# A radial coupling's last geometry operation moved from GpSimd to VectorE, and two vector products of two tiles made one

## The reference

```
R   = relu(edge_weight @ w1 + b1) @ w2 + b2              # 384 numbers per edge
Y   = spherical_harmonics(edge_attr_3)                   # 1, 3 and 5 of them
Fj  = x[src]                                             # 8 scalars, 8 vectors of 3
acc = acc + norm * einsum('euv,ef,evi,ofi->euo', R.., Y.., F.., C)   # for each pair of orders
out = zeros.at[dst].add(concat(msg_blocks))
x   = layernorm(x + out)
```

## Time and profile before

| | us |
|---|---|
| median of 3 timed runs | 20091.51 |
| lowest and highest | 20090.82, 20093.43 |
| span of the profiled execution | 25995.0 |
| radial stage in that span | 13880 to 21703 |

### The profile page before, as it was taken

One profiled execution on the slowest core, in us unless ns is written; L12 is line 12 of the kernel. 1 busy time (PEld: TensorE's weight loads), 2 busy tenths in 40 slices (PEclk: granted clock), 3 DMA queues, 4 the chain that ended last, 5 costly groups with the idle time before them and its releaser, 6 DMA issues.

```text
span 25995.0 us, 290953 instructions
## 1 busy us (share of the span) xinstructions
PE 9853.2 (38%) x63545; PEld 7350.7 (28%) x63546; DVE 16714.1 (64%) x23622; ACT 6288.5 (24%) x13799; POOL 13429.9 (52%) x14067
## 2 busy tenths in 40 slices
PE   0131000000000006765225666666666666324422
PEld 0131000000000006664223444444444444313421
DVE  9898574547344438888555666666666677555555
ACT  0002121112111105543002333333333345201400
POOL 0187676667777760000664555555555552363165
PEclk6555555555555559985556777777777776555555
DMA  1133434441000001116222000000000006424623
GB/s 14 25 33 27 29 31 29 29 29 13 6 6 6 6 15 48 41 52 227 69 69 18 9 10 9 9 9 9 9 9 9 9 10 144 137 64 87 205 65 61
DMA packets 1751558, 1095.98 MB, mean 42 GB/s; under 512 B 1217323, under 2 KB 1658124, under 8 KB 1750028
## 3 DMA queue, kind: packets, MB, share of 16 engines
q0 software_dynamic: 454272, 412.11, 13.3%
q1 hardware_dynamic: 1089532, 417.46, 6.8%
q10 hardware_dynamic: 207632, 265.14, 3.3%
HBM read 700.94 MB, written 391.12 MB: 42 GB/s over the span
## 4 chain that ended last, share of the span: by engine, by line
DVE 31%; another core or an unknown queue 21%; issue 17%; DVEq 12%; PE 11%; ACT 4%; DMA 2%; ACTq 1%; POOL 0%; SPq 0%; POOLq 0%
PE banks L1423 5%; DVE arena L1768 5%; DVE arena L1767 4%; DVE red L2523 4%; DVEq L2201 3%; DVE hot L2196 2%; DVE arena L1740 2%; DVE arena L2207 2%; DVE srcs L2516 2%; PE banks L1365 2%; PE banks L1410 2%; DVEq L498 1%; DVE arena L1585 1%; DVEq L2261 1%
## 5 line engine op out<-in xcount | busy, mean ns | idle before, releaser
L804 POOL DMA_INDIRECT srcs<-spread,nbx x2808 | 2653.2, 945 | 5691.9 <-issue 3372.8
L782 POOL DMA_INDIRECT gat<-tab,nbr x3328 | 3455.0, 1038 | 2537.8 <-issue 1271.9
L1423 PE MATMUL banks<-w2rows,dsts 128*128 128x384 f32 x6656 | 3443.8, 660 | 1030.2 <-DVE srcs L2516 699.0
L782 POOL DMA_INDIRECT gat<-tab,pay x3328 | 3161.6, 950 | 1077.4 <-issue 892.0
L748 POOL DMA_INDIRECT pay<-records,nbr x2560 | 2746.2, 1073 | 843.1 <-issue 827.1
L1208 PE MATMUL banks<-ident,arena 128*128 128x128 f32 x2240 | 436.2, 379 | 7154.4 <-DVE arena L1768 2837.8
L909 ACT COPY banks<-arena 128x1024 f32<-128x1024 f32 (+1 forms) x1508 | 1318.6, 875 | 6430.8 <-issue 2701.9
L2511 DVE TENSOR_TENSOR srcs<-banks,g_s 128x512 f32<-128x512 f32 x1664 | 1146.1, 689 | 2252.6 <-remote 1505.1
L1208 PEld LDWEIGHTS banks<-ident,arena 128*128 128x128 f32 x2240 | 400.7, 204 | 7190.5 <-DVE arena L1768 2844.2
L2523 DVE TENSOR_REDUCE red<-srcs 128x160 f32<-128x2560 f32 x832 | 2346.2, 2820 | 75.6
L1279 PE MATMUL banks<-srcs,hot 128*128 128x96 bf16 (+1 forms) x11232 | 1169.8, 281 | 3175.7 <-DVE hot L2196 2136.8
(11 more groups left out here) (392 smaller groups left out, 22029.8 us busy)
## 6 DMA issues: line engine op xcount, KB each, us to landing
spread<-srcs SPq DMA_DIRECT2D x936, 192.0 KB, 2.9
dsts<-key_rows SPq DMA_DIRECT2D x234, 512.0 KB, 4.1
spread<-srcs ACTq DMA_DIRECT2D x468, 204.0 KB, 2.4
staged<-gat SPq DMA_DIRECT2D x416, 148.0 KB
gat<-staged ACTq DMA_DIRECT2D x416, 148.0 KB, 2.1
dsts<-key_rows ACTq DMA_DIRECT2D x117, 512.0 KB, 4.3
gat<-tab,nbr POOLq DMA_INDIRECT x3328
gat<-tab,pay POOLq DMA_INDIRECT x3328
```

Source lines behind the costliest of these rows:

```text
L782: pool.indirect_dma_start(out=gatv(s, GC[pas])[:, t, :], out_offset=None, in_=TAB[pas], in_offset=bass.IndirectOffsetOnAxis(ap=row, axis=0 ...
L804: pool.indirect_dma_start(out=chunk_rows(s, c)[:, q, :], out_offset=None, in_=rows, in_offset=bass.IndirectOffsetOnAxis(ap=nbx[:, r, s * X ...
L1423: last = t_.matmul(bank[1 + 2 * (p % 2) + h][:, 0:384], hid_rows[:, s % 2, 2 * p + h, :], w2rows[:, :], start=True, stop=True)
```

## The change

GpSimd's geometry keeps tmpA and tmpB; the subtraction goes to VectorE, after tmpC's product and before g_s's reduction. GEO_OPS is 2, VectorE waits for `geo_ops` there, and no longer between the reduction and the first pair. A new semaphore `geo_used` tells GpSimd that VectorE has read tmpA and tmpB; GpSimd waits for it before it overwrites them. The two products of lines 2516 become one of 768 elements over both tiles, with R repeated over three components and g_v over eight channels. The vector part of a message has the component first (o, then u), also in the last product and in the sums; the two additions to x read it with a stride.

```diff
-        GEO_OPS = 3
+        GEO_OPS = 2
...
-                if stage == 0:
-                    if not first:
-                        pool.wait_ge(geo_ops, n * GEO_OPS)
-                    pool.wait_ge(geo_ready, 2 * n + 1)
-                    pool.nop(nofuse=True)
-                    g.tensor_tensor(tA, fT[:, b, :, 2:5, :], r_(b, 1), ALU.mult).then_inc(geo_ops, 1)
-                    g.tensor_tensor(tB, fT[:, b, :, 1:4, :], r_(b, 2), ALU.mult).then_inc(geo_ops, 1)
-                else:
-                    pool.wait_ge(geo_ops, n * GEO_OPS + 2)
-                    pool.nop(nofuse=True)
-                    g.tensor_tensor(g_v[:, b, :, :, 8:16], tA, tB, ALU.subtract).then_inc(geo_ops, 1)
+                if not first:
+                    pool.wait_ge(geo_used, n)
+                pool.wait_ge(geo_ready, 2 * n + 1)
+                pool.nop(nofuse=True)
+                g.tensor_tensor(tA, fT[:, b, :, 2:5, :], r_(b, 1), ALU.mult).then_inc(geo_ops, 1)
+                g.tensor_tensor(tB, fT[:, b, :, 1:4, :], r_(b, 2), ALU.mult).then_inc(geo_ops, 1)
...
+                dve.wait_ge(geo_ops, (n + 1) * GEO_OPS)
+                v.tensor_tensor(g_v[:, b, :, :, 8:16], tA, tB, ALU.subtract).then_inc(geo_used, 1)
                 dve.drain()
                 v.tensor_reduce(g_s[:, b, :, 8:16], tmpC[:, :, :].rearrange("p t (v o) -> p t v o", o=3), AX.X, ALU.add)
                 dve.drain()
-                dve.wait_ge(geo_ops, (n + 1) * GEO_OPS)
...
-                    for h in range(2):
-                        last = v.tensor_tensor(
-                            prod[:, f0 + h, 16:40, :].rearrange("p (u o) k -> p u o k", o=3),
-                            bank[lo + h][:, 256:384].rearrange("p (u a k) -> p u a k", a=1, k=16).to_broadcast([P, 8, 3, 16]),
-                            g_v[:, b, t0 + h:t0 + h + 1, :, :].to_broadcast([P, 8, 3, 16]), ALU.mult)
-                    last.then_inc(r_used, 1)
+                    v.tensor_tensor(
+                        prod[:, f0:f0 + 2, 16:40, :].rearrange("p t (o u) k -> p t o u k", o=3),
+                        banks[:, lo:lo + 2, 256:384].rearrange("p t (a u k) -> p t a u k", a=1, k=16).to_broadcast([P, 2, 3, 8, 16]),
+                        g_v[:, b, t0:t0 + 2, :, :].rearrange("p t o (a k) -> p t o a k", a=1).to_broadcast([P, 2, 3, 8, 16]),
+                        ALU.mult).then_inc(r_used, 1)
...
-            v.tensor_tensor(x[:, :, 8:F], x[:, :, 8:F], a2[:, :, 8:F], ALU.add)
+            xv = x[:, :, 8:F].rearrange("p w (u o) -> p w u o", o=3)
+            v.tensor_tensor(xv, xv, a2[:, :, 8:F].rearrange("p w (o u) -> p w u o", o=3), ALU.add)
```

More of the change, by code:

```diff
@@ L445, in resnorm_gnn_kernel @@
         geo_ops = sem("geo_ops")
+        geo_used = sem("geo_used")
         r_ready = sem("r_ready")
@@ L512, in sort_held @@
             return flat[:, lo:lo + (1 << (log - 2))].rearrange("p (x m l) -> p x m l", x=x, m=m)
-        GEO_OPS = 3
+        GEO_OPS = 2
+        tA, tB = [t[:, :, :].rearrange("p t (o v) -> p t o v", o=3) for t in (tmpA, tmpB)]
         @block.sync
@@ L810, in r_, with geometry @@
                 return rx[:, b, :, lo:lo + 3].rearrange("p t (o a) -> p t o a", a=1).to_broadcast([P, TPS, 3, 8])
-            tA, tB = [t[:, :, :].rearrange("p t (o v) -> p t o v", o=3) for t in (tmpA, tmpB)]
-            def geometry(n, s, stage, first=False):
+            def geometry(n, s, first=False):
                 b = s % 2
-                if stage == 0:
-                    if not first:
-                        pool.wait_ge(geo_ops, n * GEO_OPS)
-                    pool.wait_ge(geo_ready, 2 * n + 1)
-                    pool.nop(nofuse=True)
-                    g.tensor_tensor(tA, fT[:, b, :, 2:5, :], r_(b, 1), ALU.mult).then_inc(geo_ops, 1)
-                    g.tensor_tensor(tB, fT[:, b, :, 1:4, :], r_(b, 2), ALU.mult).then_inc(geo_ops, 1)
-                else:
-                    pool.wait_ge(geo_ops, n * GEO_OPS + 2)
-                    pool.nop(nofuse=True)
-                    g.tensor_tensor(g_v[:, b, :, :, 8:16], tA, tB, ALU.subtract).then_inc(geo_ops, 1)
+                if not first:
[4 more added lines that the diff above has]
+                g.tensor_tensor(tB, fT[:, b, :, 1:4, :], r_(b, 2), ALU.mult).then_inc(geo_ops, 1)
             def radial_gather():
@@ L836, in step @@
                     if geo:
-                        for stage in range(2):
-                            geometry(n + 1, s1, stage)
+                        geometry(n + 1, s1)
                     if gathers:
@@ L845, in radial_gather @@
                     gather_step(PASS_L2, 0, s, True)
-                for stage in range(2):
-                    geometry(0, 0, stage, first=True)
+                geometry(0, 0, first=True)
                 for s in range(SLOTS):
@@ L2524, in radial_step @@
                         dve.drain()
-                v.tensor_tensor(red[:, b, :, 41:CR].rearrange("p t (u o) -> p t u o", o=3),
-                                rx[:, b, :, 0:3].rearrange("p t (a o) -> p t a o", a=1).to_broadcast([P, TPS, 8, 3]),
-                                red[:, b, :, 0:8].rearrange("p t (u a) -> p t u a", a=1).to_broadcast([P, TPS, 8, 3]),
+                v.tensor_tensor(red[:, b, :, 41:CR].rearrange("p t (o u) -> p t o u", o=3),
+                                rx[:, b, :, 0:3].rearrange("p t (o a) -> p t o a", a=1).to_broadcast([P, TPS, 3, 8]),
+                                red[:, b, :, 0:8].rearrange("p t (a u) -> p t a u", a=1).to_broadcast([P, TPS, 3, 8]),
                                 ALU.mult).then_inc(msg_ready, 1)
@@ L2543, in _ @@
             v.tensor_tensor(x[:, :, 0:8], x[:, :, 0:8], a2[:, :, 0:8], ALU.add)
-            v.tensor_tensor(x[:, :, 8:F], x[:, :, 8:F], a2[:, :, 8:F], ALU.add)
+            xv = x[:, :, 8:F].rearrange("p w (u o) -> p w u o", o=3)
+            v.tensor_tensor(xv, xv, a2[:, :, 8:F].rearrange("p w (o u) -> p w u o", o=3), ALU.add)
             v.tensor_copy(dinv[:, :], a2[:, :, F])
             dve.drain()
-            v.tensor_tensor(x[:, :, 8:F], x[:, :, 8:F], a2[:, :, F + 1:C2], ALU.add)
+            v.tensor_tensor(xv, xv, a2[:, :, F + 1:C2].rearrange("p w (o u) -> p w u o", o=3), ALU.add)
             dve.wait_ge(tab_sent, 32)
```

## The result

The changed kernel takes 19,876.95 us (19,871.05 to 19,880.46 in four runs), the kernel before 20,091.58 us: a ratio of 0.9892, 95% interval 0.988 to 0.9904. That is 214.6 us less. The forecast was 20,062 us and its range ended at 19,905 us, so it was wrong by 185 us, and the range missed the time by 28 us.

The account below looks back on a forecast made before the run. VectorE with TensorE's waits (14.8 us a step) was taken as the pace, GpSimd (14.15 us) close behind. VectorE's terms, 0.27 - 0.09 - 0.25 = -0.07 us over 416 steps, gave 20091.5 - 29 = 20,062 us; range 19,905 to 20,145 us.

Parts of the forecast that it names:

- The recording's stalls: Profiled span: 25995.0 us against 20091.5 timed; some 5,460 us of unnamed waits taken as added by recording, not the kernel's.
- The last steps: End of the radial stage, without late gathers: 15.67 us a step less 0.9 unnamed, said to confirm 14.8 us.
- VectorE with TensorE's waits is the pace, GpSimd close behind: Radial step: VectorE 13.66 us plus 1.2 of TensorE's waits, 14.8 us; GpSimd 14.15, some 0.65 to spare.
- Rival (a): Radial step: GpSimd paces the timed runs; 0.56 us less over 384 steps, 19,877 us; chance 21%.
- a fall by over 100 us: Whole time: such a fall would make the prediction wrong and mean that GpSimd was the pace.
- I leave the sum as it is: TensorE's matmuls: bank release 0.12 us later; late third pairs lose about 0.05 instead of winning 0.07, kept for the range.
- Rival (b): TensorE falls to its low clock more often; at one step in twenty 95 us, 20,157 us, slower; chance 11%.
- VectorE's terms: VectorE's step: subtraction 0.27, wait removed -0.09, four merged products -0.25; sum -0.07 us a step, -29 us.
- Rival (c): VectorE: merge gives least, subtraction costs most; up to +92 us, 20,184 us, in the middle 20,122; chance 9%.
- (d): VectorE: every merge saves its fixed part in full, -0.14 us each; -0.30 a step, -125 us, 19,967 us; chance 3%.
- GpSimd's terms: GpSimd's geometry: 0.72 us less, 13.43 us a step, worth nothing while another engine paces; new geo_used wait costs nothing.
- TensorE's clock falls behind a pause before the third pair: TensorE's pause before a step's third pair: 1.38 us, growing by 0.12; in slow spells VectorE waits 4.55 us together.

Follow-up runs that it names:

- no_subtract: The kernel before with GpSimd's subtraction left out, VectorE untouched: 20,081 us, ratio 1.0004.
- before_warm4: The kernel before with five unused 384-column matmuls a step added on TensorE and nothing else: 20,051 us, ratio 0.9989.
- nosub_warm4: The kernel before with GpSimd's subtraction left out and five unused matmuls a step added on TensorE: 19,900 us, ratio 0.9913.
- tiny_extra: The changed kernel with one more 8-element product on VectorE in each step: 20,072 us as the median, ratio 1.0012.
- after_warm: The changed kernel with two unused 384-column matmuls a step added on TensorE: 19,863 us, ratio 0.9892.
- ahead_warm: The changed kernel with VectorE's next-step geometry moved ahead of the last reduction, plus two unused matmuls a step: 19,776 us, ratio 0.9849.
- before_again: The kernel before, unchanged, recorded and timed a second time: 20,083 us, ratio 1.0004.
- dve_extra_warm4: The changed kernel with tmpC's product made twice on VectorE and five unused matmuls a step on TensorE: 19,984 us, ratio 0.9956.
- ahead: The changed kernel with VectorE's geometry of the next step moved ahead of the current step's last reduction: 19,858 us, ratio 0.989.
- merge_relieved: The kernel before with the merged, component-first product and GpSimd's subtraction left out altogether: 19,868 us, ratio 0.9894.
- after: The changed kernel itself, against the kernel before: 19,877 us, ratio 0.9892.
- move_only: The kernel before with only the subtraction moved to VectorE, the pairs of products left as two: 20,107 us, ratio 1.0017.
- dve_extra: The changed kernel with tmpC's product made a second time on VectorE into a scratch buffer: 20,169 us, ratio 1.0043.

## Why the prediction was wrong, point by point

**The recording's stalls.** Right that they are no part of the kernel: recorded again, the span is 20,076 us. Wrong was the conclusion drawn from the rest of that trace. I took TensorE's waits in the disturbed stretch (445.7 us over 370 steps, 1.2 us a step) as those of the timed runs. Recorded again, they are 159.8 us over 353 steps, 0.45 us a step: in the recording with the stalls they were nearly three times as long. So the step was 14.175 us and not 14.8 us (13.66 + 1.2, which is nearer 14.9), and the 0.65 us of room that I gave GpSimd was 0.02 us. The last steps, which seemed to confirm it, came from the same disturbed recording. This is the first step that failed, and the one on which the forecast hung.

**"VectorE with TensorE's waits is the pace, GpSimd close behind."** Half right. It was one of two limits within 0.02 us of each other (no_subtract, before_warm4: each taken away alone gives 0 and 0.1%; nosub_warm4: both give 0.9%). Rival (a) was half right in the same way. Its time, 19,877 us, is what was measured, and its step of 13.59 us is near to the 13.656 us measured, but its mechanism was GpSimd alone, and that no_subtract refutes. That the time agrees to the microsecond is luck: it took 384 steps of 0.56 us, and the runs show 415 of 0.519 us. It came near because it also supposed that TensorE stays out of the way, which proved true in the changed kernel and not in the kernel before. My sentence that a fall by over 100 us would show GpSimd as the pace claimed too much.

**"I leave the sum as it is" for TensorE's waits.** The second step that failed. I took them as a constant that the change shifts by 0.12 us at most (0.05 lost instead of 0.07 won). They went from 0.45 us a step to nothing: with GpSimd out of the way and an own step of 13.65 us in place of 13.75, the low stretches come at one place of nearly every step, where VectorE has other work. tiny_extra puts back 0.1 us and gets 0.4 us (by its median) to 0.65 us (in its profiled execution) of waits. A small term of the sum thus carried a factor of some five that no row of before showed: with GpSimd relieved in both, -0.09 us of work became -0.50 us of step (14.154 us in no_subtract, 13.656 in the changed kernel). Rival (b) had the right mechanism with the wrong sign: more low clock, where the change brought less.

**VectorE's terms.** All near. The merged product lasts 948 ns against 0.95 us worked out. The subtraction starts 0.29 us behind tmpC's product (0.27). The first product stands 0.51 us behind the reduction's start (0.5). The step without waits is 13.58 us in most steps (13.6); averaged over the loop's four, own steps went from 13.746 (nosub_warm4) to 13.654 us (after_warm): -0.09 against -0.07 forecast. Alone, these terms are worth 0.09 x 416 = 38 us, near the 29 us of the sum. Rival (c), the worst sum, did not come, and nor did (d): a pair of products took 1.01 us, the merged one takes 0.95, so 0.06 saved and not 0.14. The rule of the Trainium skill ("VectorE: DVE Perf Modes", section "The DRAIN you can't avoid"), by which (d) went, doesn't hold for these products; the same section says that an op which isn't held starts earlier, and with that the trace agrees (the subtraction starts 0.29 us behind a product that lasts 0.37 us). That the sum had no term for GpSimd's gathers was right too: beside them tmpC's product and the subtraction keep their 0.37 and 0.35 us. Only ahead_warm shows a product made longer, beside another product of GpSimd.

**GpSimd's terms.** From tmpA's start to the next gather's start it takes 1.16 us (13,010.29 to 13,011.45) against 1.89 before: 0.73 less, 0.72 forecast. That "it is worth nothing while another engine sets the pace" is right word for word, and wrong in what it was used for: GpSimd set the pace as much as VectorE did. The new wait for geo_used, costed at nothing, delays nothing in the changed kernel: no time ahead of tmpA is put down to it, and the 78.0 us that name the subtraction stand ahead of 256 gathers, 0.3 us each, as long as the gaps ahead of all other gathers.

**TensorE's clock falls behind a pause before the third pair.** Right as to place: idle 1.5 us, then 0.51. Right also as to the pause, which rival (b) saw grow by 0.12 us: the median of TensorE's gaps of over 1 us ahead of a pair's matmuls is 1.52 us in before_again and 1.64 us in the changed kernel, and yet VectorE waits less. The Trainium skill ("TensorE: Matmul & The Clock Gate", section "HAM oscillation — how this bites in real kernels") advises, for a product with few rows, to restructure the loop so that TensorE stays warm. Here unused matmuls fill the pause instead; before_warm4 and after_warm show how little that gives where another gate is shut or the low stretch is covered, nosub_warm4 and dve_extra_warm4 what it gives where it is the last one: 181 and 184 us.

## What stays open

Why a low stretch ends just behind the third pair's matmuls in one kernel and lasts a whole step in another, both behind a pause of about 1.5 us, isn't settled. What the runs show is a pattern of lengths. Kernels whose own step is 13.2, 13.5 and 13.65 us (ahead, merge_relieved, after) all come to 13.64 to 13.66 us, and the two shorter ones fill the gap with waits for TensorE; those of 13.75 to 13.95 us without GpSimd in the way (no_subtract, move_only, dve_extra) come to 14.15 to 14.37 us (tiny_extra's profiled execution to 14.49). In move_only the low stretches start 0.2 us earlier from step to step until a long one comes; in the changed kernel they keep their place. So the runs fit that the length of the step decides where the low stretches fall, but no run varied the length alone, or finely enough to say where the border lies between 13.65 and 13.75 us.

## What to carry to other kernels

Where two engines' paces lie within a per cent of each other, relieve both before judging either edit: here each of the two edits alone measured -0.1% and +0.2%, and together -1.1%. Don't cost a wait as a constant when it comes from TensorE's clock in a loop; ask where in the step the low stretches fall, and test the sensitivity with one tiny added operation and with a few unused matmuls, which cost nothing where TensorE has room. And record a profile again whose span is far above the timed runs: what remains after subtracting its stalls is not the undisturbed kernel.

## What the runs showed of the hardware beyond what was expected

- An 8-element VectorE product, about 0.1 us of a 13.65 us step, cost 195 us in 416 steps, and 48 to 62 us with TensorE kept busy; 0.27 us cost 292 to 303 us and 107 to 128 us.
- Extra TensorE work made kernels faster: five unused matmuls of 384 columns a step took 181 us off no_subtract (20,081 to 19,900), two took 82 us off ahead (19,858 to 19,776).
- The granted clock was low for a fifth of the time (0.89 on average) at no measurable cost: with 0.97 (after_warm) the ratio is the same, 0.9892.
- A VectorE product of 192 elements, both inputs in SBUF, took 0.64 us in place of 0.36 us where it started 0.1 us behind a GpSimd product of the same size and from the same tiles (ahead_warm); beside GpSimd's gathers it kept to 0.36 to 0.42 us (ahead).
- One recording stretched a span by 29% with waits that no instruction explains, and the next of the same kernel by nothing; the stretched one also nearly trebled the waits that had a name (1.2 against 0.45 us a step).
